# A graph layer on one core: group 0 taken from plain chunks of edges, x turned early, and the sum of the next messages moved between the halves of layer two

## What is computed

```python
msg = relu(x[src] + edge_attr)
agg = segment_sum(msg, dst, num_segments=50000)
h = x + agg
h = relu(relu(h @ W1 + b1) @ W2 + b2)      # 128 -> 256 -> 128
out = layernorm(x + h)                     # over the 128 features, eps 1e-5
```

## Time and profile before

| | |
|---|---|
| median of 3 runs | 479.1 us (478.18 to 479.19) |
| profiled execution | 479.27 us, span 477.6 us |
| TensorE matmul busy | 462.7 us, 97% of the span |
| VectorE busy | 413.3 us, 87% |
| ScalarE busy | 409.8 us, 86% |
| GpSimd busy | 322.3 us, 67% |
| granted TensorE clock, mean | 0.996 of full |

### The profile page before, as it was taken

One profiled execution on the slowest core, in us unless ns is written; L12 is line 12 of the kernel. 1 busy time (PEld: TensorE's weight loads), 2 busy tenths in 40 slices (PEclk: granted clock), 3 DMA queues, 4 the chain that ended last, 5 costly groups with the idle time before them and its releaser, 6 DMA issues.

```text
span 477.6 us, 9937 instructions
## 1 busy us (share of the span) xinstructions
PE 462.7 (97%) x2969; PEld 360.9 (76%) x2969; DVE 413.3 (87%) x1530; ACT 409.8 (86%) x879; POOL 322.3 (67%) x313
## 2 busy tenths in 40 slices
PE   4999999999999999999999999999999999999993
PEld 2678787787877778787787877878777787877873
DVE  5589889898898988889898898988989888898985
ACT  1358998989999898998989989899998999989885
POOL 4677767767776766767667676676767767676612
PEclk9999999999999999999999999999999999999998
DMA  4565766666666666667666666667666666666622
GB/s 138 136 190 169 206 196 199 201 199 213 187 206 197 188 209 204 204 195 202 205 201 201 197 198 203 198 191 214 200 197 204 202 201 200 193 201 196 202 77 104
DMA packets 81578, 91.02 MB, mean 191 GB/s; under 512 B 13345, under 2 KB 52004, under 8 KB 81524
## 3 DMA queue, kind: packets, MB, share of 16 engines
q1 hardware_dynamic: 71634, 70.86, 46.6%
q0 software_dynamic: 9760, 19.52, 16.5%
q10 hardware_dynamic: 130, 0.00, 0.0%
HBM read 64.74 MB, written 25.60 MB: 189 GB/s over the span
## 4 chain that ended last, share of the span: by engine, by line
PE 95%; DVE 1%; ACT 0%; issue 0%; ACTq 0%
PE h_ps L743 37%; PE h1T_ps L735 35%; PE hT_ps L725 13%; PE hT_ps L711 9%; PE h_ps L131 1%; DVE stats L529 0%; DVE z L522 0%; DVE h L510 0%; DVE mean_var L538 0%; ACTq L400 0%; ACT hT L631 0%; ACT y L656 0%; DVE window_dst L106 0%; PE h_ps L124 0%; PE spare_ps L126 0%
## 5 line engine op out<-in xcount | busy, mean ns | idle before, releaser
L99 POOL DMA_INDIRECT x_src<-in_x_dram,src_of x292 | 313.4, 1073 | 132.1 <-ACT hT L631 66.6
L743 PE MATMUL h_ps<-w_sb,h1T 128*128 128x128 f32 x1564 | 193.7, 277 | 0.1
L735 PE MATMUL h1T_ps<-hT,w_sb 128*128 128x512 f32 x392 | 184.0, 592 | 0.2 <-ACT hT L631 0.2
L743 PEld LDWEIGHTS h_ps<-w_sb,h1T 128*128 128x128 f32 x1564 | 182.6, 192 | 0.6 <-ACT h1T L637 0.6
L656 ACT ACTIVATE y<-z,shift,rstd 128x128 f32<-128x128 f32 x383 | 165.5, 481 | 0.8 <-DVE shift L549 0.8
L637 ACT ACTIVATE h1T<-h1T_ps,b_sb 128x512 f32<-128x512 f32 x196 | 134.4, 686 | 21.3 <-PE h1T_ps L735 17.4
L510 DVE TENSOR_TENSOR h<-h_ps,b_sb 128x512 f32<-128x512 f32 x98 | 67.5, 689 | 48.9 <-PE h_ps L743 48.9
L735 PEld LDWEIGHTS h1T_ps<-hT,w_sb 128*128 128x128 f32 x392 | 67.0, 191 | 46.9 <-issue 46.3
L711 PEld LDWEIGHTS hT_ps<-ident,x_sb 128*128 128x128 f32 (+1 forms) x387 | 48.4, 141 | 51.1 <-issue 51.1
L529 DVE BATCH_NORM_STATS2 stats<-z 128x6 f32<-128x128 f32 x391 | 85.3, 280 | 0.1
L631 ACT ACTIVATE hT<-hT_ps 128x512 f32<-128x512 f32 x98 | 58.4, 596 | 22.0 <-PE hT_ps L725 21.8
(11 more groups left out here) (89 smaller groups left out, 104.5 us busy)
## 6 DMA issues: line engine op xcount, KB each, us to landing
x_sb<-in_x_dram SPq DMA_DIRECT2D x97, 256.0 KB
out_dram<-y SPq DMA_DIRECT2D x97, 256.0 KB
pre_msg<-in_edge_attr_dram SPq DMA_DIRECT2D x293, 64.0 KB
x_src<-in_x_dram,src_of POOLq DMA_INDIRECT x292, 2.7
w_sb<-in_w_dram SPq DMA_DIRECT2D x2, 128.0 KB, 2.3
x_sb<-in_x_dram SPq DMA_DIRECT2D x1, 168.0 KB
out_dram<-y SPq DMA_DIRECT2D x1, 168.0 KB
dst_rows<-in_dst_dram SPq DMA_DIRECT2D x1, 97.7 KB
```

The lines of the kernel that those rows point to most:

```text
L99: nc.gpsimd.indirect_dma_start(out=c["x_src"][:, g % EB, k, :], out_offset=None, in_=x, in_offset=bass.IndirectOffsetOnAxis(ap=c["src_of"] ...
L735: nc.tensor.matmul(h1T_ps[h][:, 0:n, 0:p], w1_sb[:, h * 128:(h + 1) * 128], hT[:, 0:n, 0:p], start=True, stop=True).then_inc(h1_summed, 1)
L743: last = nc.tensor.matmul(h2_ps[g % 2][0:p, t, :], h1T[:, h, t, 0:p], w2_sb[:, h, :], start=(h == 0 and t == 0), stop=(h == HC - 1), skip_ ...
```

## The change

- **TensorE's loop:** `output_sum(g, 0)` now stands ahead of `sum_messages(g + 1)`, and `output_sum(g, 1)` behind it.
- **x early:** the messages of groups 1, 2 and 3 get banks of their own (`bank_of`), and `turn_x` of these is done before or between the first steps. SyncE loads x of group 0 ahead of the weights, x of group 1 behind them, and x of 2 and 3 at the start of `main_path`.
- **Group 0 without windows:** its edges are the first 384, in three plain chunks of 128 (`first_pairs`, loaded whole). Two gathers of x[src] start in preparation, ahead of the windows of parts 1 and 2, the third behind them; the window of part 0 is fetched in `main_path`. `select_first` builds their 0/1 matrices over all the partitions of the group from `P0[k]` on, and `sum_first` adds them, 512, 336 and 168 columns wide.
- **Smaller moves:** targets are made relative to the node range after the turn rather than before (`target_nodes`, no `window_nodes`), `source_nodes` of parts 1 and 2 goes to ScalarE, and all `keep_warm` calls but one are gone.

```diff
 def target_nodes(nc, dve, k, ps, c):
-    first = 1 if k == 0 else 0
     dve.wait_ge(c["dst_T_ready"], ORDER.index(k) + 1)
-    return nc.vector.tensor_copy(c["dst_of"][:, first:, k], ps[:, first:])
+    return nc.vector.tensor_tensor(c["dst_of"][:, :, k], ps, c["node_row"][:, k, :], ALU.subtract)
...
+            nc.gpsimd.iota(c["node_in_group"][:, :].rearrange("p (t q) -> p t q", t=T), pattern=[[1, T], [T, 128]], base=0,
+                           channel_multiplier=0, allow_small_or_imprecise_dtypes=True).then_inc(pool_consts, 1)
+
             pool.wait_ge(pairs_loaded, 16)
...
+            start_first_gather(nc, x, 0, c)
+            pool.wait_ge(more_pairs_loaded, 16)
+            start_first_gather(nc, x, 1, c)
+            for i, k in enumerate(ORDER[:2]):
                 pool.wait_ge(start_ready, i + 1)
...
+                start_window(nc, pairs, k, c)
+            start_first_gather(nc, x, 2, c)
...
         @block.gpsimd
         def _(pool):
+            pool.wait_ge(c["start_ready"], K)
+            start_window(nc, pairs, 0, c)
             pool.wait_ge(c["src_of_ready"], 1)
-            start_gather(nc, x, 0, 1, c["first_loaded"][0], c)
+            start_gather(nc, x, 1, 1, c["first_loaded"][2], c)
             pool.wait_ge(c["src_of_ready"], 2)
-            start_gather(nc, x, 0, 2, c["first_loaded"][1], c)
-            start_gather(nc, x, 1, 1, c["first_loaded"][2], c)
             start_gather(nc, x, 1, 2, c["first_loaded"][2], c)
-            pool.wait_ge(c["src_of_ready"], 3)
+            pool.wait_ge(last_src_ready, 1)
             start_gather(nc, x, 1, 0, c["first_loaded"][3], c)
...
+            def sum_first(part, k, final=False):
+
+                return nc.tensor.matmul(hT_ps[:, :, P0[k]:], part[:, 0, k, :], first_nodes(c["first_sel"][:, k, :], k),
+                                        start=False, stop=final, skip_group_check=True)
...
             pe.wait_ge(c["starts_row_ready"], 1)
             turn_window(nc, pe, 0, src_ps[0], dst_ps[0], c)
-            pe.wait_ge(targets_ready, 1)
-            for columns in (256, 256, 256, 192):
-                keep_warm(nc, columns, flat_h2[1], c)
-            pe.wait_ge(sel_ready, 1)
-            sum_messages(0)
-            for _ in range(2):
-                keep_warm(nc, 128, flat_h2[1], c)
+            turn_x(1)
+            pe.wait_ge(c["src_of_ready"], 2)
+            pe.wait_ge(last_src_ready, 1)
             hidden_sum(0)
-            turn_x(1)
+            pe.wait_ge(targets_ready, K)
+            turn_x(2)
             output_sum(0, 0)
-            sum_messages(1)
+            sum_messages(1, 0)
             output_sum(0, 1)
+            turn_x(3)
+            sum_messages(1, 1)
             for g in range(1, GROUPS):
                 hidden_sum(g)
+                if inside(g + 1) and g + 1 not in bank_of:
+                    turn_x(g + 1)
+                output_sum(g, 0)
                 if inside(g + 1):
-                    turn_x(g + 1)
                     sum_messages(g + 1)
-                for h in range(HC):
-                    output_sum(g, h)
+                output_sum(g, 1)
```

More of the change, by code:

```diff
@@ L38 @@
 EB, XB, ZB, YB, SB = 6, 6, 6, 4, 4
-X_FIRST, X_AHEAD = 3, 5
+X_FIRST, X_AHEAD = 4, 5
 GATHER_AHEAD = 3
@@ L101, in start_gather, with start_window, start_first_gather, first_nodes @@
         in_offset=bass.IndirectOffsetOnAxis(ap=c["src_of"][:, g, k:k + 1], axis=0)).then_inc(loaded, 16)
[L104 to L112, removed]
+def start_window(nc, pairs, k, c):
+    nc.gpsimd.indirect_dma_start(
+        out=c["window"][:, k, :, :].rearrange("g e a -> g (e a)"), out_offset=None, in_=pairs,
+        in_offset=bass.IndirectOffsetOnAxis(ap=c["window_start_i"][:, k:k + 1], axis=0)).then_inc(c["window_loaded"][k], 16)
+def start_first_gather(nc, x, k, c):
+    loaded = c["first_loaded"][[i for i, ks in enumerate(PARTS[0]) if ks.start <= k < ks.stop][0]]
+    nc.gpsimd.indirect_dma_start(
+        out=c["x_src"][:, 0, k, :], out_offset=None, in_=x,
+        in_offset=bass.IndirectOffsetOnAxis(ap=c["first_pairs"][:, k, 0:1], axis=0)).then_inc(loaded, 16)
+def first_nodes(tile, k):
+    return tile.rearrange("p (t q) -> p t q", t=T)[:, :, P0[k]:]
+def select_first(nc, k, c):
+    return nc.vector.tensor_scalar(first_nodes(c["first_sel"][:, k, :], k), first_nodes(c["node_in_group"], k),
+                                   c["first_dst"][:, k:k + 1], None, ALU.is_equal).then_inc(c["first_sel_ready"], 1)
 def target_nodes(nc, dve, k, ps, c):
-    first = 1 if k == 0 else 0
     dve.wait_ge(c["dst_T_ready"], ORDER.index(k) + 1)
-    return nc.vector.tensor_copy(c["dst_of"][:, first:, k], ps[:, first:])
+    return nc.vector.tensor_tensor(c["dst_of"][:, :, k], ps, c["node_row"][:, k, :], ALU.subtract)
 def turn_window(nc, pe, k, src_ps, dst_ps, c):
@@ L202, in _ @@
                          allow_slow_non_contiguous=True).then_inc(next_loaded, 16)
-            sp.dma_start(first_pairs[:, :], pairs[0:EW, :]).then_inc(pairs_loaded, 16)
+            sp.dma_start(first_pairs[:, 1:K, :], pairs[EW:K * EW, :].rearrange("(k p) a -> p k a", p=EW),
+                         allow_slow_non_contiguous=True).then_inc(more_pairs_loaded, 16)
+            start_x(sp, x, 0, 0, c)
+            for k in range(K):
+                sp.dma_start(c["pre_msg"][:, 0, k, :], edge_attr[k * EW:(k + 1) * EW, :]).then_inc(c["ea_loaded"][0], 16)
             sp.dma_start(c["w1_sb"][:, :], w1).then_inc(weights_loaded, 16)
@@ L208, in _ @@
             sp.dma_start(b2_sb[:, 0, :], b2.rearrange("(a n) -> a n", a=1).to_broadcast([128, b2.shape[0]])).then_inc(weights_loaded, 16)
-            for g in range(X_FIRST):
-                start_x(sp, x, g, g, c)
-            sp.dma_start(c["pre_msg"][:, 0, 0, :], edge_attr[0:EW, :]).then_inc(c["ea_loaded"][0], 16)
+            start_x(sp, x, 1, 1, c)
         @block.gpsimd
@@ L342, in _, with main_path @@
             nc.tensor.matmul(sums_ps, ones_col[:, :], violations[:, :], start=True, stop=True).then_inc(flags_summed, 1)
-def main_path(nc, x, edge_attr, out, c, sb, sem):
+def main_path(nc, x, pairs, edge_attr, out, c, sb, sem):
     D = x.shape[1]
@@ L421, in store @@
                 sp.dma_start(rows(out, g, c), y[:, g % YB, :, :]).then_inc(out_stored[g % YB], 16)
[L423 to L426, removed]
+            for g in range(2, X_FIRST):
+                load_x(g)
             sp.wait_ge(c["weights_loaded"], 16 * (3 + HC))
@@ L620, in _, with source_nodes @@
         def _(act):
+            def source_nodes(k):
+                act.wait_ge(c["src_T_ready"], ORDER.index(k) + 1)
+                nc.scalar.activation(src_of[:, :, k], src_ps[k], ACT.Copy).then_inc(c["src_of_ready"], 1)
             def high_part(g, i=0):
@@ L708, in turn_x, with sum_messages @@
                 for t in range(tiles(g, c)):
-                    if t == 1:
-                        pe.wait_ge(sel_ready, g + 1)
-                    nc.tensor.matmul(hT_ps[:, t, 0:p], x_sb[0:p, g % XB, t, :], ident[0:p, 0:p], is_transpose=True,
+                    if t == 1 and g not in bank_of:
+                        pe.wait_ge(sel_ready, g)
+                    nc.tensor.matmul(sum_bank(g)[:, t, 0:p], x_sb[0:p, g % XB, t, :], ident[0:p, 0:p], is_transpose=True,
                                      start=(t == 0), stop=False, skip_group_check=True)
-            def sum_messages(g):
+            def sum_messages(g, only=None):
                 bounds, n = (LP0, LT) if g == LAST else (P0, T)
+                if g in bank_of:
+                    pe.wait_ge(sel_ready, g)
                 for i, ks in enumerate(parts(g, c)):
+                    if only not in (None, i):
+                        continue
                     pe.wait_ge(msg_lo_ready, parts_to(g, c) + i + 1)
@@ L1066, in gnn_resnorm_kernel @@
         with nc.If(windows_fail == 0):
-            main_path(nc, x, edge_attr, out, c, sb, sem)
+            main_path(nc, x, pairs, edge_attr, out, c, sb, sem)
         with nc.Else():
```

102 lines of the change are left out of this document (59 added, 43 removed).

## The result

The changed kernel takes 514.88 us (median of 5 runs, 514.84 to 515.5) against 479.1 us before: ratio 1.0753, 95% interval 1.0741 to 1.0765. The profiled execution took 515.5 us, with a span of 513.9 us, 36.3 us longer than before. Each ratio in this document is taken over fast executions alone, so where executions scatter it is not the quotient of the two medians given.

The account below looks back on a forecast made before the run. TensorE (4.61 us per group) bounded the kernel before; afterwards a circle through ScalarE would. 34.3 start + 93 x 5.16 + 11.5 end = 525.7 us span, plus 1.67 = 527.4; forecast 527, range 514 to 540 (own range 518 to 538).

Parts of the forecast that it names:

- The circle: Loop: copy of hT, ScalarE's queue, hidden half 0, half 0 of layer two, messages, next copy; 5.16 us per group, 93 periods.
- Theory A: Theory in the experiments: the loop's circle through ScalarE's work between copy of hT and hidden half 0 sets the 5.00 us period.
- the rivals in which ScalarE has time to spare: Loop: copy's cover or VectorE sets the period, ScalarE spares 1.13 us per group; one more normalize leaves 515 us.
- C to the end of hidden half 0: Loop, ScalarE: from start of the copy of hT through normalizes and high part to hidden half 0's end, 2.57 + 0.69 = 3.26 us.
- lower bound of 5.10: Loop period in us if the two sets of normalizes and the hand-over run 0.06 us quicker than shown.
- PE's wait: Loop: layer two's weight load waits for ACT's hidden half over 90 times, 0.5 us each, some 50 us in all.
- The half-long cover: Loop: half 1 of layer two, 0.89 us, covers the copy of hT, 0.28 + 0.60 us; called just enough.
- C: Start of ScalarE's copy of hT in a loop group, the zero point for the times of the following steps.
- The start: Before the loop: group 1's first layer starts near 21.9 us, 3.2 us earlier; copy of group 4 at 34.3 against 37.35.
- a route through GpSimd: Start: what limits group 1; its last gather is issued at 18.65 us, its first layer starts at 25.09, 6.4 us on.
- nothing gained: Lower bound for the start: small descriptors of the added pairs load or PE's lower clock take the freed wait.
- The clock rival: Loop: PE's idle times make the clock fall; a tenth of the groups at 1.2 GHz adds 37 us, 564 in all; chance 0.04.

Follow-up runs that it names:

- one more: Changed kernel with one extra normalize per group on ScalarE behind the copy of hT: 551.58 us, ratio 1.1517.
- one less: Changed kernel without the fourth normalize of each group in the loop: 480.96 us, ratio 1.0040.
- high_first2: Changed kernel with ScalarE's high part moved directly behind the copy of hT, second run: 529.59 us beside 512.39 for the kernel before, ratio 1.039.
- two_window0: Changed kernel with two normalizes ahead of the copy of hT, high part directly behind it, part 0's window fetched in the preparation: 482.29 us, ratio 1.0069.
- order_back: Changed kernel with half 0 of layer two moved behind the next messages again (old loop order): 526.82 us, ratio 1.003.
- order_only2: Kernel before with only TensorE's loop order changed, second run: 534.98 us, ratio 1.048.
- back_window0: Changed kernel with the old loop order and part 0's window issued in the preparation, ahead of the third plain gather: 479.27 us, ratio 1.0002.
- order_back2: Changed kernel with TensorE's old loop order, taken again on another chip: 510.47 us, ratio 0.997.
- two_ahead: Changed kernel with two normalizes ahead of the copy of hT and the high part directly behind it: 539.67 us beside 528.51 for the kernel before, ratio 1.028.

## Why the prediction was right, and where it was off

- **The circle** was right in place, order and count. Theory A's numbers for one more and one less held to 1 and 2 us. The first removed the rivals in which ScalarE has time to spare; `high_first2` removed VectorE's wait for the high part, `two_window0` the short cover (but for its 3 us), and `order_back` with `order_only2` the start and the banks. The chain shows the normalizes as foretold.
- **The period was mis-sized, 5.16 against 5.00.** This is the term "C to the end of hidden half 0, 3.26 us". I had taken 0.82 us for two normalizes up to the high part and 0.83 for two up to hidden half 0 as ScalarE's own pace. They are 0.77 each (258.20 to 258.97, 259.38 to 260.15). Before, the rows ended in waits so short that the record of the instruction ahead, 0.48 us long with a pace of 0.385, still covered them and no idle time was printed. In the chain of before the first layer starts at 34.51 us, and hidden half 0, there plainly released by PE, at 35.41; at 43.74 and 44.63 it is the same distance without an idle time shown. And the high part follows its pre_msg at once: 250.31 + 0.52 = 250.83, high part at 250.87. So ScalarE waited in both places, for PE and for VectorE, and the pace that I read held their waits. That makes 0.12, and the hand-over from hidden half 0 to PE 0.72 rather than 0.75 the rest: 93 x 0.16 = 15 us too many. The period also fell below its own lower bound of 5.10, so it is not a matter of the bounds chosen: the reading of those rows was wrong.
- **PE's wait** was called 0.5 us each and 50 in all; the wait list shows 33.6. The loss is 0.39 per group: 0.34 there, and most of the rest at the copy of hT, as the next point says.
- **The half-long cover** was called just enough. The working had 0.65 against 0.61 us, and the 0.04 is real: 257.42 to 258.35 is 0.93 us where half 1 covers 0.89. In the changed kernel it costs nothing of its own, since PE waits for hidden half 0 anyway; `two_window0` shows its price.
- **VectorE**: bias at C + 0.92 (258.62) and low part at C + 1.81 (259.51) came as worked out, at C + 0.92 and C + 1.83. It costs nothing, as said.
- **The start was wrong.** The copy of group 4 was put at 34.3 us, 3 us earlier than before; it came at 37.57, 0.2 later. Group 1's first layer comes at 24.80 us against 25.09, not at 21.9. The window of part 0 is issued at 11.57 us, not 11.0, and lands 4.6 us later rather than 2.9, and then the first layer of group 0 takes 3.31 us for its records. Rows of the changed kernel's start:

```profile
16.29 0.41 PE L137 MATMUL prep_ps<-ident,window 98*128 98x98 f32 x1 [2.02 <-DMA window<-in_pairs_dram,window_start_i]
...
17.51 3.31 PE L777 MATMUL h1T_ps<-hT,w_sb 128*128 128x512 f32 x4
...
24.80 1.98 PE L777 MATMUL h1T_ps<-hT,w_sb 128*128 128x512 f32 x4 [0.69 <-ACT hT L661]
```

  The step that failed is the one that named the limit, "a route through GpSimd". Before, the messages behind the gather of 18.65 were ready at 22.89 us and PE took up that sum at 23.45: from 20.38 to 25.09 the chain lies on PE alone. In the changed kernel the chain goes from the window through PE's own list. hT of group 0 is copied by 14.90 us, but PE's list has the turn of that window ahead of group 0's first layer, so the layer stands until 17.51. From there PE runs without a wait to the sum for group 1's copy at 24.16.

  The lower bound, "nothing gained", had named the lower clock as a cause; it had not named the late window. That the layer ran at the lower clock is read from its pace: its loads stand 0.86 us apart (18.36 to 19.22) and later 0.43 (258.89 to 259.32). The granted clock of this trace reads 1.00 there, so the row of clocks doesn't bear it out; but it reads 0.50 in `one_more`, which has the same start, where the same layer takes 3.30 us. That the clock set the time of group 1 on the undisturbed chip was not tried.
- **The clock rival** is out: the granted clock is 0.998 in the profiled execution and 0.991 in the others, and the first layer's loads keep their 0.43 us in the loop, with PE waiting in every group. The rule of the Trainium skill on short idle times (TensorE: Matmul & The Clock Gate, "A second HAM failure mode: psum-queue depth-cycling") did not show here at 0.34 us per 5.0 us.
- **The sum**: 525.7 + 3.3 (start) - 14.9 (period) - 0.1 (end, 513.9 - 502.5 = 11.4) = 514.0, and the span is 513.9. Two errors of opposite sign brought the total to the edge of the range. Without the 3.3 us that the start failed to gain, the time would have been 511.6 us, outside 514 to 540: that it fell inside is luck, while the way and the place of the loss were not.

## What to carry to other kernels

Before moving a step on the busiest engine, follow each of its inputs once round: what does the engine that makes it do in between, in its own order, and is that behind something the moved step will now delay? An idle engine helps only at the place in its queue where it is idle: ScalarE had 1.1 us per group to spare and still set the pace, and two instructions moved ahead of its wait (with the window fetched early) brought back all of the loss but 3 us. When the pace of an engine is to be read, take it where the engine surely waits for nothing (four normalizes in 1.64 us, `high_first2`), not where merely no idle time is printed.

## What the runs showed that was not expected

- A pair of normalizes of 0.48 us each follow each other every 0.385 us, so a wait of up to about 0.1 us (0.48 - 0.385) leaves no idle time in the rows.
- Of the indirect transfers at the start, the sixth landed late in two kernels, and it is not the same transfer: in the changed kernel the window of part 0 lands 4.6 us after its issue, and in `back_window0`, where the window goes ahead of it, the third plain gather takes 4.6 us and the window is no longer waited for. Group 1's first layer then comes at 25.93 us rather than 24.80. What makes it late was not tried, and on another chip (`order_back2`) the same window landed after 3.7 us.
- On two of the three chips the kernel before ran 7 and 10% longer. In traces of new-order kernels there, the copy of hT starts later behind the first load of half 1 of layer two: 0.42 us in the median of `order_only2` and 0.87 in that of `two_ahead`, instead of 0.28. Why PE's release arrives later there is open.
